# A masked softmax times x on one core: x by four neighbouring rows a partition, strips transposed from every fourth word

## The reference

```
in_fts = context @ W_common.T
left   = in_fts @ w_left  + b_left          # one number a row
right  = in_fts @ w_right + b_right
logits = left[:, None] + right[None, :]
logits = where(logits >= 0, logits, 0.2 * logits)
logits = where(adj <= 0, -inf, logits)
out    = layernorm(x + relu(softmax(logits) @ x))
```

## Time and profile before

| | |
|---|---|
| three runs | 1478.53, 1478.82, 1481.78 us; median 1478.82 |
| the profiled execution | 1479.36 us, its span 1477.6 us |
| PE busy | 1376.9 us, 93% |
| DVE busy | 1306.2 us, 88% |
| ACT busy | 642.9 us, 44% |
| POOL busy | 72.5 us, 5% |
| granted TensorE clock, mean | 0.967 |
| HBM read and written | 319.29 and 8.39 MB |

### The profile page before, as it was taken

One profiled execution on the slowest core, in us unless ns is written; L12 is line 12 of the kernel. 1 busy time (PEld: TensorE's weight loads), 2 busy tenths in 40 slices (PEclk: granted clock), 3 DMA queues, 4 the chain that ended last, 5 costly groups with the idle time before them and its releaser, 6 DMA issues.

```text
span 1477.6 us, 28323 instructions
## 1 busy us (share of the span) xinstructions
PE 1376.9 (93%) x12334; PEld 1207.7 (82%) x12334; DVE 1306.2 (88%) x1156; ACT 642.9 (44%) x675; POOL 72.5 (5%) x207
## 2 busy tenths in 40 slices
PE   1047999999999999999999999999999999999998
PEld 0015888888888888888888888888888888888887
DVE  6979999898989999898989989999898989899981
ACT  0276444444444454444445444444445444444441
POOL 0003000000000000000000000000000000000000
PEclk7568999999999999999999999999999999999999
DMA  9996998989999998989999899999989898999870
GB/s 377 358 246 143 237 230 219 227 211 235 216 238 219 229 223 214 241 208 238 218 231 226 214 232 217 230 219 239 220 216 231 208 238 213 234 222 220 208 171 9
DMA packets 180752, 329.59 MB, mean 223 GB/s; under 512 B 19728, under 2 KB 36112, under 8 KB 179600
## 3 DMA queue, kind: packets, MB, share of 16 engines
q1 hardware_dynamic: 177264, 321.47, 87.8%
q10 hardware_dynamic: 3360, 6.29, 1.3%
HBM read 319.29 MB, written 8.39 MB: 222 GB/s over the span
## 4 chain that ended last, share of the span: by engine, by line
PE 91%; DVE 4%; DMA 3%; ACT 2%; issue 0%; SPq 0%; ACTq 0%; POOL 0%; POOLq 0%; DVEq 0%
PE ps L351 30%; PE ps L353 30%; PE ps L354 30%; DVE tab L525 2%; DMA T<-in_L_gnn_context_dram 1%; DMA T<-in_x_dram 1%; ACT X L399 1%; DVE T L716 1%; DVE strip L672 1%; ACT strip L428 0%; DVE X L621 0%; DVE tab L508 0%; ACT X L394 0%; PE pt L325 0%; ACTq L212 0%
## 5 line engine op out<-in xcount | busy, mean ns | idle before, releaser
L351 PE MATMUL ps<-X,T 128*128 128x257 f16 x4096 | 1122.4, 274 | 7.2 <-ACT X L399 5.2
L354 PE MATMUL ps<-X,T 128*128 128x257 f16 x4096 | 1121.8, 274 | 0.0
L353 PE MATMUL ps<-X,T 128*128 128x257 f16 x4032 | 1101.9, 273 | 0.0
L428 ACT ACTIVATE strip<-strip 128x2048 f32<-128x2048 f32 x256 | 488.9, 1911 | 498.6 <-DMA strip<-in_adj_dram 497.4
L716 DVE STREAM_TRANSPOSE T<-strip 128x2048 f32<-128x2048 f32 x256 | 590.1, 2306 | 62.8 <-PE ps L354 62.5
L672 DVE SCALAR_TENSOR_TENSOR strip<-tab,arow,strip 128x2048 f32<-128x2048 f32 x256 | 598.2, 2337 | 48.3 <-ACT strip L428 47.5
L351 PEld LDWEIGHTS ps<-X,T 128*128 128x128 f16 x4096 | 403.0, 98 | 70.9 <-ACT X L399 16.7
L354 PEld LDWEIGHTS ps<-X,T 128*128 128x128 f16 x4096 | 402.2, 98 | 50.1
L353 PEld LDWEIGHTS ps<-X,T 128*128 128x128 f16 x4032 | 394.9, 98 | 49.1
L409 ACT ACTIVATE xs<-ps,small 128x256 f32<-128x256 f32 x64 | 30.4, 474 | 143.7 <-DVE small L721 143.6
L306 POOL TENSOR_SCALAR small<-small 128x1 f32<-128x1 f32 x64 | 12.2, 191 | 1271.1 <-ACT xs L417 1271.1
(11 more groups left out here) (90 smaller groups left out, 215.9 us busy)
## 6 DMA issues: line engine op xcount, KB each, us to landing
strip<-in_adj_dram SPq DMA_DIRECT2D x1016, 256.0 KB, 4.8
xs<-in_L_gnn_context_dram SPq DMA_DIRECT2D x14, 1024.0 KB, 9.6
T<-in_L_gnn_context_dram SPq DMA_DIRECT2D x4, 2048.0 KB, 18.1
X<-in_L_gnn_context_dram SPq DMA_DIRECT2D x4, 2048.0 KB, 33.9
xs<-in_x_dram SPq DMA_DIRECT2D x64, 128.0 KB, 5.3
out_dram<-xs SPq DMA_DIRECT2D x64, 128.0 KB, 5.2
gw<-in_L_gnn_context_dram SPq DMA_DIRECT2D x2, 1024.0 KB, 20.1
strip<-in_adj_dram ACTq DMA_DIRECT2D x8, 256.0 KB, 12.3
```

The lines of the kernel that those rows point to most:

```text
L351: nc.tensor.matmul(ps[o][:, 0:D + 1], hi, X16[:, jb, 0:D + 1], start=(i == 0), stop=False)
L353: nc.tensor.matmul(ps[o][:, 0:D + 1], hi, X16[:, jb, XL:XL + D + 1], start=False, stop=False)
L354: m = nc.tensor.matmul(ps[o][:, 0:D + 1], lo, X16[:, jb, 0:D + 1], start=False, stop=(g > 0 and i == JB - 1))
L428: nc.scalar.activation(s, s, ACT.Relu, scale=KEEP).then_inc(s_m, 1)
```

## The change

Three edits hang together. Strips are transposed from every fourth word: block 4a + e takes columns 128 a + 4 p + e (EQ = 4). x is loaded to match, four neighbouring rows a partition in pieces of 4 KB. The right scores are laid out to match. For this the one transpose is replaced by a copy that doubles 64 columns of scores to 128, a transpose of those, and a selection by partition half in two operations (lower half of a quadrant, upper half) with masks from two small sums of the identity at the start. Their temporaries lie in T's first buffer.

```diff
@@ -47,7 +47,7 @@
     NLB = NG // LB
     LW = LB * SG
     NPL = 12
-    NHI = 2
+    EQ = 4
     HB = JB // 2
     WSCALE = 2.0 ** 10
     FSCALE = 2.0 ** 14
@@ -88,7 +88,7 @@
         rT = sb("rT", [P, JB])
         wcol = sb("wcol", [P, 2, HID // P])
         bias = sb("bias", [P, 2])
-        small = sb("small", [P, 80])
+        small = sb("small", [P, 96])
         y = xs2[:, 0:NY, :]
         xrow = xs2[:, NY:NY + 2, :]
         junk_row = xs2[:, NY + 2, :]
@@ -128,6 +128,7 @@
         mnq, m1, mn, nmax, c4 = small[:, 18:19], small[:, 19:20], small[:, 20:21], small[:, 21:22], small[:, 22:26]
         nb1, nb2 = small[:, 26:27], small[:, 27:28]
         mxc, diag = small[0:3, 28:29], small[0:3, 29:32]
+        upper, halves = small[:, 80:82], small[:, 82:90]
         c1, c2, bsum = small[:, 64:65], small[:, 65:66], small[:, 74:75]
         l4, S4 = small[:, 66:70], small[:, 70:74]
         lw = slice(JB, JB + LW)
@@ -150,6 +151,8 @@
         s_ctx = [sem(f"context_in{s}") for s in range(NCH)]
         s_lc = sem("group_context_in")
         s_const = sem("selectors_ready")
+        s_half = sem("half_masks_ready")
+        s_rq = sem("scores_by_quads")
         s_ld = sem("left_dots_done")
         s_lm = sem("left_by_strip_ready")
         s_lb = sem("left_on_all_quadrants")
@@ -209,8 +212,8 @@
 
         def x_quarter(queue, c, q):
             j0, j1 = XCH[c]
-            queue.dma_start(xrows(j0, j1 - j0)[q * B:(q + 1) * B, :, :].rearrange("p (a b) d -> p a (b d)", b=2),
-                            x[q * NQ + j0 * B:q * NQ + j1 * B, :].rearrange("(a p b) d -> p a (b d)", p=B, b=2)).then_inc(s_x[c], 16)
+            queue.dma_start(xrows(j0, j1 - j0)[q * B:(q + 1) * B, :, :].rearrange("p (a b) d -> p a (b d)", b=EQ),
+                            x[q * NQ + j0 * B:q * NQ + j1 * B, :].rearrange("(a p b) d -> p a (b d)", p=B, b=EQ)).then_inc(s_x[c], 16)
 
         @block.sync
         def _(sp):
@@ -501,6 +504,10 @@
             nc.vector.tensor_reduce(R[:, 0, :], ident[:, :].rearrange("p (q i) -> p i q", q=Q), AX.X,
                                     ALU.add).then_inc(s_const, 1)
             nc.vector.tensor_reduce(S4, ident[:, :].rearrange("p (q i) -> p q i", q=Q), AX.X, ALU.add).then_inc(s_const, 1)
+            nc.vector.tensor_reduce(halves, ident[:, :].rearrange("p (c m) -> p c m", m=B // 2), AX.X,
+                                    ALU.add).then_inc(s_half, 1)
+            dve.wait_ge(s_half, 1)
+            nc.vector.tensor_reduce(upper, halves.rearrange("p (q h) -> p h q", h=2), AX.X, ALU.add).then_inc(s_half, 1)
             dve.wait_ge(s_const, 1)
             nc.vector.tensor_copy(R[:, 1:Q, :], R[:, 0:1, :].broadcast_to([P, Q - 1, B])).then_inc(s_const, 1)
 
@@ -539,8 +546,25 @@
             dve.wait_ge(s_dot, JB)
             nc.vector.tensor_reduce(mx2[:, 0:1], r[:, :], AX.X, ALU.max).then_inc(s_stat, 1)
             nc.vector.tensor_reduce(mx2[:, 1:2], r[:, :], AX.X, ALU.min, negate=True).then_inc(s_stat, 1)
-            nc.vector.transpose(rT[:, :].rearrange("p (c h) -> p h c", h=NHI),
-                                r[:, :].rearrange("p (c h) -> p h c", h=NHI)).then_inc(s_lr, 1)
+            r2 = Thalf[0][:, 0:EQ * B]
+            r4 = Thalf[0][:, EQ * B:2 * EQ * B]
+            rq = Thalf[0][:, 2 * EQ * B:2 * EQ * B + JB]
+            nc.vector.tensor_copy(r2.rearrange("p (e s m) -> p e s m", e=EQ, s=2),
+                                  r[:, :].rearrange("p (m e s) -> p e s m", e=EQ, s=1).broadcast_to(
+                                      [P, EQ, 2, B // 2])).then_inc(s_rq, 1)
+            dve.wait_ge(s_rq, 1)
+            nc.vector.transpose(r4.rearrange("p (e a) -> p e a", e=EQ),
+                                r2.rearrange("p (e i) -> p e i", e=EQ)).then_inc(s_rq, 1)
+            dve.wait_ge(s_rq, 2)
+            dve.wait_ge(s_half, 2)
+            nc.vector.tensor_scalar(rq.rearrange("p (a e) -> p a e", e=EQ),
+                                    r4.rearrange("p (e a s) -> p s a e", e=EQ, s=2)[:, 1, :, :], upper[:, 1:2], None,
+                                    ALU.mult).then_inc(s_rq, 1)
+            dve.wait_ge(s_rq, 3)
+            nc.vector.scalar_tensor_tensor(out=rT[:, :].rearrange("p (a e) -> p a e", e=EQ),
+                                           in0=r4.rearrange("p (e a s) -> p s a e", e=EQ, s=2)[:, 0, :, :],
+                                           scalar=upper[:, 0:1], in1=rq.rearrange("p (a e) -> p a e", e=EQ),
+                                           op0=ALU.mult, op1=ALU.add).then_inc(s_lr, 1)
             dve.wait_ge(s_bc, 1)
             nc.vector.tensor_reduce(mxc[0:2, :], pt[0:2, P:2 * P], AX.X, ALU.max).then_inc(s_amx, 1)
             dve.wait_ge(s_amx, 1)
@@ -713,8 +737,8 @@
                 if k == 0 and (not isinstance(g, int) or g >= 2):
                     dve.wait_ge(s_mm, g - 1)
                 dve.wait_ge(s_p, n + 1)
-                nc.vector.transpose(T[:, o, :, k * B:(k + 1) * B].rearrange("p (a e) i -> p a e i", e=2),
-                                    strip[:, b, :].rearrange("p (a i e) -> p a e i", i=B, e=2)).then_inc(s_t, 1)
+                nc.vector.transpose(T[:, o, :, k * B:(k + 1) * B].rearrange("p (a e) i -> p a e i", e=EQ),
+                                    strip[:, b, :].rearrange("p (a i e) -> p a e i", i=B, e=EQ)).then_inc(s_t, 1)
 
             def reciprocal(g, o):
                 dve.wait_ge(s_mm, g + 1)
```

## The result

The changed kernel took 1755.34 us (median of 4 runs, 1754.07 to 1759.29) against 1478.67 for the one before: ratio 1.1876, 95% interval 1.186 to 1.1893. It is 277 us slower. The profiled execution has a span of 1752.2 us, 274.6 more than before.

The account below looks back on a forecast made before the run. TensorE bounded at 21.10 us a group; VectorE would take over at 27.80. Group 1 ready at 146.0, plus 62 groups, TensorE's last group 21.1, clock 2.6, end 6.15 and 1.76 around: 1901 us, 29% slower; range 1474 to 1960.

Parts of the forecast that it names:

- likeliest case: Strips' transposes on VectorE: a 16-byte read step adds 1.04 ns a word, time 1901 us, range 1840 to 1960; chance 0.45.
- rival 2: Strips' transposes: the 16-byte step costs 0.66 ns a word, 1.36 us a transpose, giving 1703 us; chance 0.17.
- What bounds, and the point from which it decides: Steady groups: TensorE bounds at 21.10 us; VectorE has 0.46 us a strip to spare, beyond which it becomes the bound.
- The price of 16 bytes: Strips' transposes on VectorE: reading every fourth word adds 1.04 ns a word, 2.13 us a transpose, 4.44 us in all.
- the row that was put second: L501 against L503: sums of 128 words, 128 bytes apart or adjacent, 361 against 276 ns, so 0.66 ns a word.
- The extra beat: Strips' transposes: one more 1.04 ns a word, as if each read needed its own access.
- Head: Start until group 1 is transposed: VectorE's fourth transpose ends at 93.9 us, factors +1.4, group 1 +8.5, ready at 146.0.
- 4 KB pieces: Loading of x at the start: 2048 fewer pieces save 0 to 2.0 us on the last landing.
- fixed part of 15.8 ns: DMA packets: cost of each packet whatever its length, from 2 KB at 90.2 ns and 16 KB at 611 ns.
- The first rival: Strips' transposes: the step of four words is free, TensorE still bounds, 1477.4 to 1479.4 us; chance 0.25.
- The scores: Right scores at the head: four new operations replace a 236 ns transpose, delaying the head 0.8 us (bounds 0 and 1.2).
- The clock: TensorE's last group: after a pause it starts at half clock, adding 2.6 us (0 to 2.6).

## Why the prediction was right or wrong

The changed kernel was forecast slower, by a free step made dear and VectorE made the bound, and it was. The time, 1755, lies in the stated range, which says little, since 1474 to 1960 held both signs. It does not lie in the likeliest case's own range (1840 to 1960): it falls between rival 2 (1703) and the forecast (1901).

That own range was worked out wrongly. It was said to be 0.75 to 1.3 ns a word. By the prediction's own sum 0.75 ns (1.54 us a transpose, a group of 25.40 us) gives 1748 us and 1.3 ns gives 2036; 1840 to 1960 answers to 0.93 to 1.15 ns only. The measured 0.79 ns lies within the prices named, and 1755 within the times that they give.

- **What bounds, and the point from which it decides: right.** VectorE's 0.46 us to spare a strip were passed, all its waits went, TensorE waits once a group. The transpose at 12 bytes adds 2956 - (169 + 2016 x 1.042) = 0.69 us, and that kernel is slower too.
- **The price of 16 bytes: the mis-sized term.** It was taken as one more beat, 2.13 us a transpose; it is 1.58 on the queue (1.61 in the duration), 0.79 ns a word in place of 1.04. With 1.58 the prediction's own sum gives a group of 19.26 + 6.32 = 25.58 us, measured 25.48. The 0.55 us x 4 x 62 = 136 us are nearly all of the 146 by which 1901 is too high. The bounds (0 and 1.7 ns) held. The better yardstick was the row that was put second: L501's 0.66 ns, a far step read by the same engine from the same memory (the transposes at its 128 bytes cost (3758 - 2304) / 2048 = 0.71 ns a word more). The extra beat had no row for it.
- **Head: wrong, and small.** It was to be VectorE's fourth transpose at 93.9. With the lower price VectorE was done at 82.48 + 7.57 = 90.05 and waited 4.84 us for x: L621 starts at 94.89, late by 2.4 because of x. Group 1 was ready at 144.80 against 146.0 forecast, and that is luck in part: a transpose too dear by 0.55 us made up for x, which was later and not sooner.
- **4 KB pieces: the sign was wrong.** At most 2.0 us were to be saved; alone they cost 3.6. The fixed part of 15.8 ns was worked out from 2 KB packets of x and 16 KB packets of context. The two differ in more than length: context goes to all 128 partitions, and in x's stretch strips share the queues. The sum also held the order of transfers fixed, but `gw` came 10.6 us sooner. Which of these made the sign is open. And the 1 KB pieces, 4096 packets more, should have cost 4.0 us by it; measured was +0.06% or 0.9 us, with an interval of -0.4 to 2.2. The first rival's "2.0 off or none", with a free step, would have been missed as well: 1481.9 is what remains of the change without the transposes.
- **The scores: near, but their delay is not seen.** The four operations take 261, 311, 274 and 322 ns (estimated 278, 303, 248, 248), 1.17 us in place of 1.08. Of the 0.8 us by which they were to delay the head nothing shows beyond the scatter: after them VectorE was no later at its fourth transpose (83.36 against 84.52 us, with the transposes' step at two). The groups by shape:

```profile
L564 DVE SCALAR_TENSOR_TENSOR rT<-T,small 128x64 f32<-128x64 f32 x1 | 0.3, 322 | 0.0
L556 DVE STREAM_TRANSPOSE T<-T 128x128 f32<-128x128 f32 x1 | 0.3, 311 | 0.0
...
L560 DVE TENSOR_SCALAR T<-T,small 128x64 f32<-128x64 f32 x1 | 0.3, 274 | 0.0
...
L552 DVE COPY T<-r 128x128 f32<-128x128 f32 x1 | 0.3, 261 | 0.0
```

- **The clock: 2.6 us too many in the last group.** The term had bounds of 0 and 2.6 and was taken at the upper. The granted clock was 1.00 (2.4 GHz) in the last group, which took 1746.16 - 1724.78 = 21.4 us. TensorE had paused only 1.16 us ahead of it (idle before L354 at 1724.83), since VectorE's last two transposes, at 1717.10, had no masking between them. A longer pause did bring the clock down: TensorE waited 5.75 us until 582.34, and in 579.4 to 586.2 us the clock was 0.50 (1.2 GHz). In 400 to 800 us it was 0.95 in the mean; there it cost nothing at the end, since VectorE set the pace.

## What to carry to other kernels

Before a layout changes an access pattern, count the 16-byte lines that the innermost run enters for each word, on the read and on the write, on every engine that walks it. In VectorE's transposes up to half a line a word was free, 0.75 made a word dearer by a third, a whole line by three quarters. Compare the price with what the engine has to spare in a group, not with what the edit saves elsewhere: 2 us at the head were hoped for here, against 1.6 us in each of 256 transposes. And when a cost by packet is derived from two kinds of transfer, make sure that they differ in length alone, and look which later transfer starts sooner once the queue that issues them is free sooner. Last, when a range is given as prices, put both ends through the sum.

## What the runs showed of the hardware

- A transpose of 2048 words on VectorE: 2.30 us at steps of 4 and 8 bytes, 2.96 at 12 (2016 words), 3.91 at 16, 3.90 at 32, 3.76 at 128; 3.89 with a step of 16 bytes on the write.
- With steps of 16 bytes, read and written, VectorE's masking went from 2.34 to 4.04 us (its operand in PSUM stepped too) and ScalarE's mask from 1.91 to 4.01.
- x to 32 partitions a DMA, by piece: 1 KB 336 GB/s, 2 KB 345 to 363, 4 KB 305 to 318, 8 KB 266, in 61 to 71 us, where strips share the queues (all transfers counted); end times 1478.5, 1478.0, 1481.6 and 1491.4 us. The cause isn't settled, and longer pieces also let SP ask for other data sooner.
- DMAs whose source had the outer dimension 4 used 4 of the 16 DMA engines, and x landed at about 101 GB/s: 62 us slower.
- TensorE's granted clock was 0.50 behind a pause of 5.75 us between two groups and 1.00 behind one of 1.16 us.
